# Turning a normalised block by DMA instead of on TensorE, with the last product two steps behind

## What is computed

```python
x = x + L0(x)   # gates, causal EMAs, two projections, layer norm
x = x + einsum('bti,bio->bto', x, W1[cat]) + b1
h = relu(x @ A1 + a1);  z = x + h @ A2 + a2
x = x + (z - mean(z)) * rsqrt(var(z) + eps) * gamma + beta     # L2
x = x + einsum('bnh,boh->bno', x, W3[subj]) + b3
```

## Time and profile before

| | |
|---|---|
| median of 3 runs | 754.29 us (753.92 to 754.69) |
| the profiled execution | 753.31 us |
| its span in the trace | 751.4 us |
| TensorE busy | 742.9 us |
| VectorE busy | 536.7 us |
| ScalarE busy | 364.8 us |
| GpSimd busy | 113.2 us |
| DMA queue of SyncE | 81.57 MB |

### The profile page before, as it was taken

The page is one execution under the profiler, slowest core; times in us unless marked ns, Lnnn a source line. Parts: engine busy times, 40 slices in busy tenths (PEclk is TensorE's granted clock), DMA queues, the critical chain, the costliest instruction groups (busy, mean ns, idle before and its releaser), DMA issues.

```text
span 751.4 us, 10452 instructions
## 1 busy us (share of the span) xinstructions
PE 742.9 (99%) x3421; PEld 605.6 (81%) x3421; DVE 536.7 (71%) x790; ACT 364.8 (49%) x546; POOL 113.2 (15%) x222
## 2 busy tenths in 40 slices
PE   7999999999999999999999999999999999999997
PEld 6888888888888888788888788888888888888885
DVE  5598895695695595596587589866877767666645
ACT  4373346445436535535535543656563553635331
POOL 2000040030022013004004024124301021010110
PEclk9999999999999999999999999999999999999999
DMA  8863008916934953962971872526144131331002
GB/s 263 227 188 38 28 1 117 189 59 103 187 73 82 190 92 69 185 109 56 169 138 34 135 223 83 197 85 224 58 153 150 46 127 57 127 113 68 28 35 79
DMA packets 93068, 86.17 MB, mean 115 GB/s; under 512 B 61631, under 2 KB 75998, under 8 KB 90990
## 3 DMA queue, kind: packets, MB, share of 16 engines
q1 hardware_dynamic: 91662, 81.57, 45.4%
q10 hardware_dynamic: 1184, 4.23, 1.6%
q0 software_dynamic: 192, 0.00, 0.1%
HBM read 33.33 MB, written 25.20 MB: 78 GB/s over the span
## 4 chain that ended last, share of the span: by engine, by line
PE 98%; DVE 1%; DMA 0%; issue 0%; ACT 0%; DVEq 0%; ACTq 0%
PE pc L630 13%; PE pc L628 13%; PE pc L629 13%; PE pm L628 6%; PE pm L629 6%; PE pm L630 6%; PE pt L628 6%; PE pt L630 6%; PE pt L629 6%; PE pm L747 4%; PE pm L746 4%; PE pm L745 4%; PE pm L635 3%; PE pt L635 3%; PE pm L877 1%; PE pm L878 1%
## 5 line engine op out<-in xcount | busy, mean ns | idle before, releaser
L628 PE MATMUL pc<-x_h,wg_h 128*128 128x512 f32 x224 | 88.5, 395 | 0.1
L630 PE MATMUL pc<-x_h,wg_l 128*128 128x512 f32 x224 | 88.0, 393 | 0.0
L629 PE MATMUL pc<-x_l,wg_h 128*128 128x512 f32 x224 | 87.7, 391 | 0.0
L1443 DVE TENSOR_TENSOR_SCAN stage_b<-alpha,carry,stage_b 128x512 f32<-128x512 f32 x64 | 78.4, 1267 | 0.0
L628 PE MATMUL pm<-wo_h,s_h 128*128 128x512 f32 x128 | 50.7, 396 | 0.0
L1119 ACT ACTIVATE ctx_t<-ctx_t,col_all 128x512 f32<-128x512 f32 x32 | 23.1, 723 | 56.6 <-DVE ctx_t L1423 56.6
L630 PE MATMUL pm<-wo_h,s_l 128*128 128x512 f32 x128 | 50.5, 395 | 0.0
L629 PE MATMUL pm<-wo_l,s_h 128*128 128x512 f32 x128 | 50.5, 395 | 0.0
L747 PE MATMUL pm<-t_h,wt_l 128*128 128x512 f32 x128 | 50.5, 395 | 0.0
L746 PE MATMUL pm<-t_l,wt_h 128*128 128x512 f32 x128 | 50.4, 394 | 0.0
L745 PE MATMUL pm<-t_h,wt_h 128*128 128x512 f32 x128 | 50.4, 394 | 0.0
(11 more groups left out here) (248 smaller groups left out, 1932.3 us busy)
## 6 DMA issues: line engine op xcount, KB each, us to landing
x_planes<-x_pairs SPq DMA_DIRECT2D x52, 256.0 KB, 7.4
xt_scratch<-x_t SPq DMA_DIRECT2D x8, 1024.0 KB, 10.2
n_scratch<-stage_a SPq DMA_DIRECT2D x8, 1024.0 KB, 10.1
ctx_t<-xt_scratch SPq DMA_DIRECT2D x16, 512.0 KB, 6.6
x_pairs<-n_scratch SPq DMA_DIRECT2D x14, 512.0 KB, 5.3
out_dram<-x_tok SPq DMA_DIRECT2D x28, 256.0 KB, 2.0
mod<-mod_scratch ACTq DMA_DIRECT2D x8, 512.0 KB, 3.6
stage_b<-in_L_cond_weight_dram SPq DMA_DIRECT2D x2, 1024.0 KB, 5.6
```

The source lines that it names most:

```text
L628: nc.tensor.matmul(acc, ah, bh, start=start and q == 0, stop=False)
L629: nc.tensor.matmul(acc, ah, bl, start=False, stop=False)
L630: last = nc.tensor.matmul(acc, al, bh, start=False, stop=stop and q == n - 1)
L1443: nc.vector.tensor_tensor_scan(tr[:, m % 2, :], alpha[:, 1 + d:2 + d].to_broadcast([P, BLK]), tr[:, m % 2, :], carry[:, D - d, m:m + 1], A ...
```

## The change

n2 of blocks 1 to 6 no longer goes through TensorE. ScalarE normalises all four tiles of such a block (in the next step), SyncE issues four DMA transposes from stage_a to x_planes and four spreading DMAs from x_planes to stage_b, ScalarE weaves the halves to words in x_planes, and VectorE adds x2 in place. Blocks 0 and 7 are still turned on TensorE. L3 of a block now comes two steps behind its L1. The copy with beta is gone: beta is added where x3 is split. All the loops of the second stage but GpSimd's are written out.

```diff
+            def turn_n2(j):
+                sp.wait_ge(x3_hi, j * NC)
+                sp.wait_ge(x3_lo, j * NC)
+                for k in range(TILES):
+                    sp.wait_ge(n2_act, n2_acts(j - 1) + k + 1)
+                    sp.dma_start(n2_pairs16[:, :, k * P:(k + 1) * P], stage_a[:, k, :].bitcast(U16),
+                                 transpose=True).then_inc(n2_turned, 16)
+            def spread_n2(j):
+                sp.wait_ge(n2_turned, j * 64)
...
+                for half in range(2):
+                    for s in range(2):
+                        sp.dma_start(n2_planes16[64 * s:64 * s + 64, :, half, :],
+                                     n2_pairs16[half::2, s::2, :]).then_inc(n2_spread, 16)
...
+            for i in range(2, NBLK):
+                turn_n2(i - 1)
+                spread_n2(i - 1)
...
+                store_out(i - 2, 0)
+                store_out(i - 2, 1)
+                if i + 2 < NBLK:
+                    load_y(i + 2)
+                store_out(i - 2, 2)
+                store_out(i - 2, 3)
```

TensorE (the waits of `l3_tile` and `xx_product`, the general step and the tail):

```diff
+                if turns_y(j + 2) and k < 3:
+                    pe.wait_ge(n2_act, n2_acts(j + 1))
+                elif turns_y(j + 2):
+                    pe.wait_ge(y_sum, (j + 3) * NC + 3)
+                elif j == LAST - 1 and k >= 2:
+                    pe.wait_ge(n2_act, n2_acts(LAST))
+                    pe.wait_ge(n2_dve, 4)
+                elif j == LAST - 1 and k == 0:
+                    pe.wait_ge(out_ready, j * TILES - 1)
+                else:
+                    after(pe, out_ready, j * TILES + max(k - 1, 0))
...
+                if k < 3 and i >= 2 and turns_y(i):
+                    pe.wait_ge(out_ready, (i - 2) * TILES + k + 1)
...
+            def step2(i):
+                l1_product(i, b, 0)
+                l1_product(i, b, 1)
...
+                l1_product(i, b, 2)
+                l1_product(i, b, 3)
...
+                l3_tile(i - 2, 0)
+                w1_product(i, b)
+                l3_tile(i - 2, 1)
+                l3_tile(i - 2, 2)
+                for k in range(TILES):
+                    xx_product(i, b, k)
+                l3_tile(i - 2, 3)
+            def last_blocks():
+                l3_tile(LAST - 1, 0)
+                l3_tile(LAST - 1, 1)
+                turn_n2(LAST)
+                l3_tile(LAST - 1, 2)
+                l3_tile(LAST - 1, 3)
```

ScalarE, whose second copy of an x2 chunk goes to x_t for even and to soma for odd blocks:

```diff
+                if i >= 2:
+                    act.wait_ge(xx_mm, (i - 1) * TILES)
+                    act.wait_ge(x3_sum, (i - 1) * NC)
...
+                if i == 3:
+                    x2_parts(i, 0)
+                    x3_hi_part(1, 0)
+                    x3_hi_part(1, 1)
+                    x2_parts(i, 1)
+                    x3_hi_part(1, 2)
+                    x3_hi_part(1, 3)
                     normalise(i - 1, 0)
                 else:
+                    if i > 3:
+                        for m in range(NC):
+                            x3_hi_part(i - 2, m)
+                    x2_parts(i, 0)
+                    normalise(i - 1, 0)
+                    x2_parts(i, 1)
+                normalise(i - 1, 1)
+                normalise(i - 1, 2)
+                x2_parts(i, 2)
+                normalise(i - 1, 3)
+                x2_parts(i, 3)
...
+                relu_part(i)
+                for m in range(NC):
+                    weave_n2(i - 1, m)
```

VectorE:

```diff
+                j = i - 2
+                if j == 1:
+                    x2_lo_part(i, 0)
+                if j >= 1:
+                    for m in range(NC):
+                        x3_lo_part(j, m)
+                if j != 1:
+                    x2_lo_part(i, 0)
+                if more and not turned:
+                    y_sum_part(i + 1, 0)
+                x2_lo_part(i, 1)
...
+                output(j, 2 if j == 0 else 0)
+                hid_lo_part(i)
+                output(j, 3 if j == 0 else 1)
+                if i == LAST:
+                    for m in range(NC):
+                        x3_sum_part(i - 1, m)
                     x3_lo_part(i - 1, 0)
                     x3_lo_part(i - 1, 1)
+                if j > 0:
+                    output(j, 2)
+                if i == LAST:
                     x3_lo_part(i - 1, 2)
                     x3_lo_part(i - 1, 3)
...
                 for k in range(TILES):
                     norm2_stats(i, k)
+                if i < LAST:
+                    for m in range(NC):
+                        x3_sum_part(i - 1, m)
+                if j > 0:
+                    output(j, 3)
```

More of the change, by code:

```diff
@@ L614, in _ @@
             l3_residual(1)
[L615 to L618, removed]
+            with pool.Fori(1, NBLK) as j:
                 norm2_scale(j)
@@ L895, in l3_product, with turn_n2 @@
[L895 to L903 removed]
+            def turn_n2(j):
+                pe.wait_ge(n2_act, n2_acts(j))
+                pe.wait_ge(n2_dve, 2 if j == 0 else 4)
+                for c in range(NC):
+                    turn(n2_bank(j, c), [stage_a[:, k, out_cols(c)] for k in range(TILES)]).then_inc(tn_done, 1)
@@ new lines, in l3_tile, with first_step2 @@
+                for c in range(NC):
+                    if k == 0:
+                        pe.wait_ge(x3_hi, j * NC + c + 1)
+                        pe.wait_ge(x3_lo, j * NC + c + 1)
+                    last = product(l3_bank(j, k)[:, :], [(ch[:, c, tok], cl[:, c, tok], wh[:, c, :], wl[:, c, :])],
+                                   start=(c == 0), stop=(c == NC - 1))
+                last.then_inc(l3_mm, 1)
+            def first_step2():
+                for m in range(1, NC):
+                    l1_product(1, 0, m)
+                turn_n2(0)
+                w1_product(1, 0)
+                pe.wait_ge(l3_hi, NC)
+                pe.wait_ge(l3_lo, NC)
+                l3_tile(0, 0)
+                l3_tile(0, 1)
+                pe.wait_ge(relu_done, 2)
+                turn_l3(1, 0, pc[0])
+                turn_l3(1, 1, pc[1])
+                xx_product(1, 0, 0)
+                xx_product(1, 0, 1)
+                pe.wait_ge(out_ready, 2)
+                turn_l3(1, 2, pt[0])
+                turn_l3(1, 3, pt[1])
+                xx_product(1, 0, 2)
+                xx_product(1, 0, 3)
@@ L1330, in _ @@
             subject_hi(0, 3, pt[1])
[L1331 to L1333 removed]
+            relu_part(0)
             for k in range(TILES):
@@ L1730, in step2 @@
-                if last:
-                    output(i - 1, bp, 3)
+                if i < LAST:
+                    for m in range(NC):
+                        x3_sum_part(i - 1, m)
+                if j > 0:
+                    output(j, 3)
             y_sum_part(0, 2)
@@ new lines, in _ @@
+            x3_lo_part(0, 0)
+            x3_lo_part(0, 1)
+            x3_sum_part(0, 2)
+            x3_sum_part(0, 3)
+            x3_lo_part(0, 2)
+            x3_lo_part(0, 3)
+            hid_lo_part(1)
+            for c in range(NC):
+                y_lo_part(2, c)
+            output(0, 0)
+            output(0, 1)
+            subject_lo(1, 0, pc[0])
+            subject_lo(1, 1, pc[1])
+            for k in range(TILES):
+                norm2_stats(1, k)
+            subject_lo(1, 2, pt[0])
@@ L1776, in _ @@
+            subject_lo(1, 3, pt[1])
+            adapter_lo(1)
+            for i in range(2, NBLK):
+                step2(i)
+            normalise(LAST, 2)
+            normalise(LAST, 3)
+            output(LAST - 1, 0)
+            output(LAST - 1, 1)
+            x3_sum_part(LAST, 0)
+            x3_sum_part(LAST, 1)
             x3_lo_part(LAST, 0)
-            x3_sum_part(LAST, 1, 2)
+            x3_sum_part(LAST, 2)
             x3_lo_part(LAST, 1)
-            x3_sum_part(LAST, 1, 3)
+            x3_sum_part(LAST, 3)
```

517 lines of the change are left out of this document (211 added, 306 removed).

## The result

The changed kernel takes 756.55 us, the median of nine runs (755.19 to 757.28). The kernel before takes 754.53 on the same chips, nine runs (752.85 to 756.04). The ratio is 1.0025, with a 95% interval of 1.0015 to 1.0036: slower by 2.0 us by the medians (1.9 by the ratio), where +1.0 was forecast. The profiled run took 755.83 us with a span of 754.0, against 753.31 and 751.4 before; that pair is 2.5 apart (2.6 in the spans).

A forecast was written before the change was run, and what follows sets the result against it. TensorE, busy 99% of the span, was taken as the bound. Terms -12.2 + 4.4 + 2.5 + 6.2 + 0.1 = +1.0 us on the median of 754.29 gave 755.3 us, range 747 to 760.

The forecast's parts named there:

- Removed, -12.2: TensorE's turns of blocks 1 to 6 go (-10.6 us) and the old tail's gaps shrink (-1.6 us).
- The detour: Blocks 1 to 6: DMA transposes, spread and weaves; 10.8 us from the spread's first issue to its last landing.
- Item 1: Step 3: L1 chunks 2 and 3 wait for x2_lo, 2.2 and 2.1 us; +4.4 us, bounds 2 and 6.
- Item 2: Steps 4 to 7: VectorE's output 2 waits for a store queued behind the spread; +2.5 us, bounds 0 and 6.
- Rival B: Steps 4 to 7: the small store passes the spread, so item 2 alone falls; 752.8 us, chance 0.10.
- Item 3: Tail: TensorE waits for output 2, output 3 and the last normalise; +6.2 us, bounds 3.5 and 9.
- Item 4: Work costed at nothing, except the seam, where turn_l3 comes sooner and may meet GpSimd's add_eye: +0.1 us.
- Rival A: Blocks arrive about 3 us earlier, as a spread without a 1 MB store behind it goes faster; 746.8 us, chance 0.18.
- Rival C: Steps 4 to 7: the y load holds back the spread by 1.5 us; 761 us, chance 0.18 with the clock's case.
- The bounds: The bounds of the three items (step 3, steps 4 to 7, tail) together: 747.7 to 763.5 us.

The follow-up runs named there:

- run with half a spread: Kernel after, issuing only the two spread DMAs of the high halves, weaves waiting for two DMAs instead of four: 747.45 us, ratio 0.991 to the kernel before.
- run with slots: Kernel after, with outputs 2 and 3 of blocks 1 to 6 in two slots of their own (tile gate): 754.53 us, ratio 0.9999 to the kernel before.

## Why the prediction came out as it did

The forecast of 755.3 us (slower by 1.0) was 1.3 us low. The mechanism was right for the detour and most of what it makes late; one term, the seam, was mis-sized and one cause misread. That the sum came so near is in part luck, since the seam's miss was offset by items 1 and 2.

- **Removed, -12.2.** 96 instructions are gone and so are the two old gaps of the tail. TensorE's busy time fell to 735.7, not to 732; 1.6 of the 3.4 is the slow clock. The rest is how busy time is drawn: of each of the six gaps 0.16 us counts as busy (1.77 lost, 1.61 idle), and the losses of 0.2 to 0.4 count whole, 1.8 together. The run with half a spread bears the size out: 754.5 - 12.2, and 1.27, 2.14 and 1.5 for the seam, step 3 and the tail, make 747.2, or 747.6 with the 0.39 ahead of W1, and 747.45 was measured.
- **The detour, 10.8 us from the spread's issue to the weave.** 10.6. Right.
- **Item 1, step 3, +4.4.** 3.9. The size was right, but its second part (2.14) is no effect of the detour, as I had bounded it "by a spread that lands 2 us sooner or later": it stays with half a spread and with none, and goes with another order.
- **Item 2, steps 4 to 7, +2.5.** 1.9 in the trace and 2.0 by the run with slots. The number held, in other places than said: 1.43 in step 4 for 0.9, and 0.4 in steps 5 and 6 for 1.6, where the profile was lucky. And the cause was misread. I put the store "behind the spread in the same queue", and it takes as long on another queue. Rival B, that the store passes the spread, fails too.
- **Item 3, tail, +6.2.** 2.01 and 2.71 and then 1.6 of slow clock make 6.3, where 2.3, 2.8 and 1.1 were summed. The first two are the waits that were named. The third is another than foreseen, and that the sum fits is luck: the seven slow matmuls took the place of the wait for the last normalise, which profiles of other runs show instead (1.06). I had given the clock's fall little. The Trainium skill ("TensorE: Matmul & The Clock Gate", part 1) says that an idle TensorE is put to half its clock. The gap of 2.71 here agrees; the same gap in the run with the slots had a granted clock of 1.00 behind it.
- **Item 4, seam, +0.1.** 1.27 and 0.39, so 1.7. This is the term that was mis-sized. I had looked there at the meeting with add_eye, and the cost is that two sums of VectorE stand ahead of x2 and x3 and run beside linear_lo. Items 1 and 2 came out 1.1 smaller in exchange. The terms as measured sum to -12.2 + 13.8 = +1.6, and the medians say +2.0. In the profiled pair the stretch from block 0's turn to the end grew by 1.8 (754.0 - 520.40 against 751.4 - 519.56), so the terms leave 0.2 of it. The turn itself stands 0.8 later, ahead of all that the prediction looks at; in the other runs it lies between 520.15 and 522.10, and why it moves is open.
- **Rival A, the block 3 us earlier, 746.8.** It didn't happen: the spread takes 10.3 to 10.7 us in all six blocks. Its price was near, since the split spread brings the block 3.4 us earlier, at 747.95, but not by its terms: the seam's 1.7 was not in it and the tail lost 1.8 where it had 3.2. Rival C (761) found no y load in the way: the spread takes 10.7 and 10.6 us in steps 6 and 7, which have none.
- **The bounds.** The upper bounds of the three items give 763.2, not 763.5; nothing hangs on it.

## What to carry over

A transfer in a chain with no slack is best cut so that its first consumer can start on a part: eight DMAs with two semaphores gave 8.6 us where the four with one had lost them, in part because the transfer itself became shorter. Edits on one late chain don't add up: test them together as well as alone, since a gap closed ahead of a late chain (+2.4 us alone) pays only once the chain itself is earlier. Before an operation of VectorE with two SBUF inputs is moved, look at what GpSimd does at that time.

## What was not expected of the hardware

- TensorE's clock fell behind some gaps and not behind others of the same length. A gap of 2.14 us in step 3 was followed by eight slow matmuls in the run without the detour and by none in the run with half a spread. The windows of the first, then of the second:

```profile
572.50:574.40 1.90, 0.00 (x0) 1.00 0.02 4
574.40:577.70 3.30, 3.24 (x8) 0.55 0.00 0
```

```profile
571.50:573.40 1.90, 0.00 (x0) 1.00 0.07 16
573.40:576.70 3.30, 3.24 (x14) 1.00 1.04 194
```

  What decides it no run here shows; it adds about 1.6 us to a gap where it happens.
- GpSimd's chain of nine operations on 128x4 tiles, 2.9 us in the tail before, took 6.0 us in step 4 (596.46 to 602.50) beside VectorE's sums and x3_lo, which read only SBUF there. ScalarE's first normalise of the step waited 1.52 us for it, and TensorE lost nothing there.
- The 1 MB spread takes 8.8 to 9.8 us as eight DMAs and 10.3 to 10.7 as four, with rows of the same length, from the first issue to the weave that needs all of it.
